# Taking the throttle off indirect DMAs: scatters and gathers of a job issue without waiting for the ones ahead

## The reference

```
x = x + attn_a(norm(x))   # multi-scale convolution with gains, per head
x = x + ffn(norm(x))      # first pass
x = x + attn_b(norm(x))   # recurrence h = tanh(h A^T + x_t B^T), y = h C^T, over t
x = x + ffn(norm(x))      # second pass, same weights
```

```
top1 = argmax(x @ Wg.T)
for e in range(8):
    y = gelu(x @ W1[e] + b1[e]) @ W2[e] + b2[e]     # 128 -> 512 -> 128
    out = where(top1 == e, y, out)
```

## Time and profile before

| | |
|---|---|
| median of three runs | 1378.8 us (1377.97 to 1391.76) |
| profiled execution | 1384.0 us; its span, first to last instruction, 1382.0 us |
| mean granted clock of TensorE | 0.926 of 2.4 GHz |
| PE busy | 1201.2 us, 87% (of it 304.4 us the dummies of line 1129) |
| PEld busy | 1011.5 us, 73% |
| DVE, ACT busy | 775.3 us, 56%; 662.4 us, 48% |
| POOL busy | 795.5 us, 58% |
| gathers, line 925 | 128, 974 ns of POOL each |
| scatters, line 908 | 80 and 48, 1002 and 988 ns each |
| DMA | 110.15 MB, mean 80 GB/s |

### The profile page before, as it was taken

One profiled execution on the slowest core, in us unless ns is written; L12 is line 12 of the kernel. 1 busy time (PEld: TensorE's weight loads), 2 busy tenths in 40 slices (PEclk: granted clock), 3 DMA queues, 4 the chain that ended last, 5 costly groups with the idle time before them and its releaser, 6 DMA issues.

```text
span 1382.0 us, 29713 instructions
## 1 busy us (share of the span) xinstructions
PE 1201.2 (87%) x8225; PEld 1011.5 (73%) x8225; DVE 775.3 (56%) x1760; ACT 662.4 (48%) x2087; POOL 795.5 (58%) x1274
## 2 busy tenths in 40 slices
PE   3999998999989989997899888999968899889883
PEld 2767677777767768775678767788868889878773
DVE  4888776888867878865664656743321223203311
ACT  2332331556425746753457546565623468326431
POOL 2565548355767868865738457676554553354442
PEclk9999999999999999998889989997978889879996
DMA  4700002222011222222223222223442244315552
GB/s 126 226 1 1 1 2 61 70 66 81 25 48 47 66 65 76 61 62 81 67 73 97 85 59 67 78 71 87 132 129 63 60 119 138 112 51 155 148 157 73
DMA packets 120652, 110.15 MB, mean 80 GB/s; under 512 B 15876, under 2 KB 90669, under 8 KB 120493
## 3 DMA queue, kind: packets, MB, share of 16 engines
q1 hardware_dynamic: 109728, 90.77, 23.5%
q0 software_dynamic: 8192, 16.79, 4.0%
q10 hardware_dynamic: 2573, 0.69, 0.2%
HBM read 79.02 MB, written 29.16 MB: 78 GB/s over the span
## 4 chain that ended last, share of the span: by engine, by line
PE 60%; DVE 10%; issue 8%; POOL 7%; another core or an unknown queue 6%; ACT 5%; ACTq 1%; DMA 1%; DVEq 1%; POOLq 0%
PE bank L1250 11%; PE bank L1237 11%; PE bank L1129 10%; PE bank L1276 6%; POOL acc L885 5%; PE bank L1173 4%; PE bank L1200 3%; DVE made L1399 2%; PE bank L1141 2%; DVE term L1428 2%; PE bank L1116 2%; PE bank L1230 2%; PE bank L1214 1%; ACT hT L1071 1%
## 5 line engine op out<-in xcount | busy, mean ns | idle before, releaser
L885 POOL TENSOR_TENSOR acc<-acc,term 128x512 f32<-128x512 f32 x219 | 286.3, 1307 | 39.2 <-DVE term L1428 13.4
L1129 PE MATMUL bank<-esel 128*128 128x256 f32 x1718 | 304.4, 313 | 3.7 <-issue 3.7
L1129 PEld LDWEIGHTS bank<-esel 128*128 128x128 f32 x1718 | 251.4, 205 | 28.9 <-issue 25.8
L1276 PEld LDWEIGHTS bank<-hid,abcT 128*128 128x128 f32 x1024 | 172.7, 208 | 92.3 <-ACT hid L1091 49.3
L1071 ACT ACTIVATE hT<-bank,b1T 128x128 f32<-128x128 f32 x596 | 179.0, 372 | 105.5 <-PE bank L1237 74.0
L1250 PE MATMUL bank<-w,hT 128*128 x1192 | 200.1, 299 | 20.4 <-ACT hT L1071 15.4
L1276 PE MATMUL bank<-hid,abcT 128*128 128x16 f32 x1024 | 173.5, 246 | 41.6 <-ACT hid L1091 26.3
L1091 ACT ACTIVATE hid<-bank 128x16 f32<-128x16 f32 x512 | 94.1, 184 | 237.2 <-PE bank L1276 175.7
L1250 PEld LDWEIGHTS bank<-w,hT 128*128 128x128 f32 x1192 | 167.8, 204 | 36.6 <-issue 32.7
L1428 DVE TENSOR_TENSOR term<-bank,V 128x512 f32<-128x512 f32 x251 | 165.9, 681 | 42.9 <-PE bank L1200 17.4
L1399 DVE SCALAR_TENSOR_TENSOR made<-bank,qkvb,K 128x512 f32<-128x512 f32 x251 | 171.8, 741 | 27.8 <-PE bank L1173 11.1
(11 more groups left out here) (176 smaller groups left out, 2079.7 us busy)
## 6 DMA issues: line engine op xcount, KB each, us to landing
w1b<-in_W SPq DMA_DIRECT2D x122, 256.0 KB
K<-in_W SPq DMA_DIRECT2D x69, 256.0 KB
xsb<-sorted_x SPq DMA_DIRECT2D x191, 64.0 KB
sorted_y<-ysb SPq DMA_DIRECT2D x149, 64.0 KB
X<-in_x SPq DMA_DIRECT2D x64, 64.0 KB
out_x<-X SPq DMA_DIRECT2D x64, 64.0 KB
sorted_x<-K SPq DMA_DIRECT2D x14, 256.0 KB, 3.7
sorted_y<-made SPq DMA_DIRECT2D x42, 64.0 KB
```

Of the source, the lines that this page charges most:

```text
L885: nc.gpsimd.tensor_tensor(acc[:], acc[:] if k > 1 else term[0][:], term[k % NTERM][:], ALU.add).then_inc(S["terms_added"], 1)
L1129: nc.tensor.matmul(bank[b][:, 0:256], tile(esel, 0), esel[:, 0:256], start=True, stop=True, skip_group_check=True)
L1276: nc.tensor.matmul(bank[6 + u][:, k * NB:(k + 1) * NB], abcT[:, 0:D], prev, start=False, stop=True, skip_group_check=True).then_inc(S["ste ...
```

## The change

The two waits in POOL's queue go, and so do the three constants and the clause in lag() that told the planner of them. No instruction is added. The costs in PACE and LANDS stay, and so does hop(), so every piece keeps its rank; only the times at which pieces become ready change. From the first piece whose time changes, the emitted order of all engines may differ, and the count of dummies with it. Semaphores, buffers and the waits for data are as before.

```diff
-TOGETHER = 3
-LIMIT_SCATTER, LIMIT_GATHER = 4, 3
...
-TABLE_US, LOOK_US, DAWDLE, LANDED_US = 1.283, 0.15, 50.0, 0.3
+TABLE_US, LOOK_US, DAWDLE = 1.283, 0.15, 50.0
...
 def lag(todo, x, y):
 
     if todo[x].engine != todo[y].engine:
         return hop(todo, x, y)
-    what, n, k = y
-    if x[0] == what and (what == "scatter" and n >= LIMIT_SCATTER or what == "gather" and n >= LIMIT_GATHER):
-        if k and k % TOGETHER == 0:
-            return todo[x].took + LANDS[what] + LANDED_US
     return todo[x].pace
...
                 elif what == "scatter":
...
-                    if n >= LIMIT_SCATTER and k and k % TOGETHER == 0:
-                        c, q = divmod(k - 1, TPC)
-                        pool.wait_ge(scattered[n % 2][q], tiles_scattered(n) - 16 * (JOB[n].chunks - c - 1))
...
                 elif what == "gather":
...
-                    if n >= LIMIT_GATHER and k and k % TOGETHER == 0:
-                        c, q = divmod(k - 1, TPC)
-                        c += CHUNKS_BEFORE[n]
-                        pool.wait_ge(back_in[c % 2][q], 16 * (c // 2 + 1))
```

## The result

The change makes the kernel **slower**: 1427.3 us (median of four runs, 1425.2 to 1432.0) against 1383.2 us for the kernel before beside it, a ratio of 1.033 with a 95% interval of 1.028 to 1.038. Predicted were 1361 us, 1342 to 1385. Both the sign and the range were wrong here. What the change does in each case is the subject of this document.

The account below looks back on a forecast made before the run. In the last 500 us the recurrence, TensorE's slots and the scatter feeding them were taken to alternate as the bound. Savings of 6.6 + 11 = 17.6 us off the 1378.8 us median gave 1361 us, range 1342 to 1385.

Parts of the forecast that it names:

- three in flight is no limit of the queue: POOL's indirect DMAs: unthrottled, each still takes 1 us of POOL; later landings were taken as 0, at most 3.46 us.
- job 0's thirteen scatters: Evidence on unthrottled chains: they leave from 207.08 to 223.00 us, 1.33 us apart, each taking 1 us of POOL.
- A wait that is met already costs nothing: POOL's queue: 28 of the 47 waits had been met when POOL reached them, so their removal changes nothing.
- Part 1: End of the kernel, job 8: removing two scatter waits and two gather waits saves 6.6 us on the path.
- the scatters' term: Job 8's two scatter waits: 3.55 us saved, unless the dummy matmuls stay 78 and hide it.
- The gathers' term: Job 8's two gather waits, before the output stores: 3.08 us saved.
- The estimate that was made from it: By the skill's latency, two chain ends come up to 1.8 us later each, leaving 3 us for job 8's gain.
- Parts 2 and 3: Last scatters of job 7 leave 16.6 us earlier, of job 6 14 us earlier; about a third, 11 us, reaches the end.
- The point of divergence: Planned order: everything before job 3's fourth gather, the first throttled issue, stays unchanged in order and time.
- the slower one: Rival: job 6's earlier slots slow the recurrence, chunk 11 taking 43.2 instead of 25.2 us; 1390 us, chance 0.16.
- if the time from the last scatter to its xsb load grows: Warning sign on a job's scatters and the SP loads that follow: if seen, the predicted sum is wrong.

Follow-up runs that it names:

- g1: Kernel before with its instruction order kept and all 47 POOL waits for its own landings removed, on the slow kind: 1.030 of the kernel before.
- e8: The kernel before, unchanged, run for a trace on the slow kind: 1371 us.
- e1: Kernel before with its order kept and all 47 POOL waits for its own landings removed, on the fast kind: 0.994 of the kernel before.
- f1: Repeat in a later set: order of before, all 47 waits removed, on the fast kind: 0.994 of the kernel before.
- e3: Order of before, waits ahead of gathers removed, those ahead of scatters kept, on the fast kind: 0.993 of the kernel before.
- f3: The changed kernel (new order, no waits) run on the fast kind: 0.987 of the kernel before.
- e5: The changed kernel (new order, no waits) run again on the slow kind: 1.030 of the kernel before.
- f4: The changed kernel with a POOL pause of 2.9 us in each of the 47 wait places, on the fast kind: 1.070 of the kernel before.

## Why the prediction was wrong

- **The step that failed** is the claim of what a chain does without the wait: "three in flight is no limit of the queue", with the bounds "nothing, or all of the longest wait seen, 3.46 us" for a later landing. The bound was for POOL's own transfers only. The price fell on the other engines, which the sum put at nothing without a reason: in scatters and gathers after 900 us PE's idle time grew from 15.1 and 22.5 to 34.9 and 42.7 us between the two profiles, and from 8.2 and 10.9 to 14.5 and 12.5 us between 400 and 900, together 48 us where the span grew by 43. g1 shows the mechanism with the order unchanged: the missing waits alone, priced at -6.6 us, cost 3.0%, some 40 us.
- **The evidence that misled** was job 0's thirteen scatters. I read them on POOL alone. Had I read the other engines, I would have seen no stall either: in 207 to 223 us PE is busy for 14.10 of 16 us, so the row below would have supported the same wrong bound. Why that chain is harmless on the slow kind stays open. It runs beside three weight loads and an attention part, not beside the recurrence, and one long chain in one place was taken for all.

```profile
207.00:223.00 16.00, 14.10 (x86) 10.79 (x85) 11.19 (x24) 2.51 (x4) 12.25 (x12) 1.00 0.32 95
```

- **What the trace of before did show** and I passed over: the place-in-chain table can be made from it. In chains that the wait does not break (a wait already met, or scatters and gathers alternating) PE's idle share at the seventh to ninth place is 0.61 in the very trace that I had read (0.56 in e8). "A wait that is met already costs nothing" was true; that a wait which is not met may be worth something was not asked.
- **Part 1, the wait's own price:** 6.6 us predicted, of 1384. On the fast kind, where no stall covers it, e1 and f1 won 0.56% and 0.64%, 7 and 8 us. Right in sum, and in part by luck, for the split looks wrong: e3, which leaves the scatters' waits in, won the same 0.66%. These times alone can't settle it, since the scatters' term is 0.28% and the intervals are 0.3% to either side. The trace of f1 speaks for it: there are still 78 dummies, which the part had named as what would hide this term, and SP's first xsb load of job 8 comes 12 us after the last scatter, behind two weight loads that it issued when the dummies had ended.

```profile
1175.49 0.97 POOL L908 DMA_INDIRECT sorted_x<-V,slot_i  x1 [0.30 <-issue]
...
1175.87 9.60 PE L1129 MATMUL bank<-esel 128*128 128x256 f32 x78
...
1185.64 1.52 SPq L815 DMA_DIRECT2D K<-in_W  x2
1187.36 4.64 SPq L823 DMA_DIRECT2D xsb<-sorted_x  x6
```

  The gathers' term was too small, 3.1 us against 8 (5 to 12) for all gathers; that the waits in gathers ahead of job 8 cost the rest is a guess. The Trainium skill gives an HBM access latency of 2 us at high load (DMA: Bandwidth & Descriptors, Latency and other measured facts). The estimate that was made from it, 3 us for this part, did not show: the measured gains are more than twice that, though e1's interval, from 2.6 us, does not rule it out.
- **Parts 2 and 3, the order:** job 7's scatters did shrink to 19.0 us (19.05 predicted), and job 6's last one left 10.9 us earlier in f3 than in f1 (14 predicted; 976.2 against 987.1). On the fast kind the order without waits is worth 0.9865 / 0.9936, 0.7% or 9 us, where 11 were predicted; the two intervals, 0.3 to 0.4% to either side, leave it barely clear of nothing. The two profiled executions don't show it (1245.1 and 1245.3 us), so this rests on the timed runs. On the slow kind nothing of these parts can be measured beside the stall: the changed kernel (e5) and g1 both stand at 1.030.
- **The point of divergence** was put too early: the orders differ from job 4's scatters on, not from job 3's fourth gather.
- **The rivals:** the slower one (1390, the recurrence loses to earlier slots) had the recurrence longer and the sign right, by another mechanism; chunk 11 did take 33.3 us instead of 25.2, but with PE idle, not full of slots. None of the rivals had other engines stop while POOL issues. The warning sign named last, "if the time from the last scatter to its xsb load grows", is what came: 20.4 us instead of 2.4.

## What to carry to other kernels

A wait whose idle time looks like pure loss may be what lets the other engines work: before removing it, look at the others' idle time by its place within the engine's unbroken stretches, not only at the engine that waits. Break a chain of indirect DMAs from GpSimd after about three with a microsecond of other work of POOL; that needs no landing and was 2.4% better than the waits on the kind of chip that stalls (the new order with short pauses, and short pauses on the fast kind, were not run). Keep the pause short: with pauses of 2.9 us the new order lost 8% on the fast kind (f4 against f3). And a tuned order belongs to its waits: the same order is 1.3% faster without them and 2.3% slower with them on one kind, and 3% slower without and 2% faster with them on the other.

## What the runs showed of the hardware that was not expected

- Two kinds of chip, or of condition: the kernel before takes 1255 to 1257 us on one and 1371 to 1387 us on the other, with mean granted clocks of 0.970 to 0.982 and of 0.921 to 0.936 (its runs beside e1 and e5). Part of the difference is this stall: in all scatters and gathers after 400 us PE is idle for about 61 us in e8 and 24 us in e1, 37 of some 120 us. Where the rest comes from was not taken apart. The recurrence's matmuls, in a row of each (busy us, mean ns, idle before, releasers; before on the slow kind, then e1 on the fast), stand idle 38.2 and 3.5 us:

```profile
L1276 PE MATMUL bank<-hid,abcT 128*128 128x16 f32 x1024 | 173.2, 245 | 38.2 <-ACT hid L1091 24.4 <-issue 13.0
```

```profile
L1276 PE MATMUL bank<-hid,abcT 128*128 128x16 f32 x1024 | 162.6, 234 | 3.5 <-ACT hid L1091 3.2
```

- In a long chain on the slow kind PE, ACT and DVE stop together and SP slows down, while POOL goes on at 0.96 us for each indirect DMA and the DMA engines are less than half busy (0.36 and 0.41 where the three stand). In g1 a signal of the recurrence then takes 2.3 us instead of 0.01, and SP's short instructions 0.23 us or more instead of 0.06, while 2 KB packets of its loads keep their median of 84 ns. The Trainium skill says of such DMAs that many descriptors can be emitted before an incremental cost shows up (DMA: Bandwidth & Descriptors, Anatomy of one DMA — SWDGE (gpsimd) path). For POOL the trace agrees: in job 7 of the changed kernel the second scatter takes 0.96 us and the sixteenth 0.95. For the others it does not hold on this kind of chip. Which resource they share stays open: signals between engines and SP's own instructions slow down together, and no run separates them.
